# A cross-attention, linear-attention and mixture-of-experts layer on one core: half of each expert tile's down projection in split form, and slot-table writes in bursts

## The reference, cut to what matters

```python
x = x + xattn(layernorm(x), ctx, ctx, mask)       # 16 heads, 257 context rows
x = x + attn(layernorm(x))                        # causal linear attention
x = x + ffn(layernorm(x))
def ffn(x):                                       # 1024 tokens of 512
    shared = silu(x @ shared_wg.T) * (x @ shared_wu.T) @ shared_wd.T
    scores = sigmoid(x @ gate_w.T)
    topw, topi = top_k(scores, 8); topw = topw / topw.sum(-1)
    # 64 experts, I = 256; each token visits 8 of them
    g = silu(buf @ expert_wg); u = buf @ expert_wu
    out_buf = (g * u) @ expert_wd                 # the down projection
    return shared + sum over the 8 of topw * out_buf[expert, pos]
```

## Time and profile before

| | |
|---|---|
| median of 3 runs | 1292.07 us (1289.84 to 1292.19) |
| profiled execution, its own time | 1291.37 us |
| its span, first to last instruction | 1289.4 us |
| TensorE busy | 1225.0 us, 95% of the span |
| VectorE busy | 733.9 us, 57% |
| ScalarE busy | 594.8 us, 46% |
| GpSimd busy | 395.2 us, 31% |
| mean granted TensorE clock | 0.991 |

### The profile page before, as it was taken

How to read it: one execution, slowest core, us unless ns; L and a number is a source line. 1 busy time by engine, 2 the same in 40 slices (tenths; PEclk the granted TensorE clock), 3 DMA queues, 4 the chain that set the end, 5 groups by cost and what they waited for, 6 DMA issues and landing times. The chain is left out here.

```text
span 1289.4 us, 31822 instructions
## 1 busy us (share of the span) xinstructions
PE 1225.0 (95%) x9830; PEld 923.9 (72%) x9831; DVE 733.9 (57%) x1509; ACT 594.8 (46%) x1184; POOL 395.2 (31%) x312
## 2 busy tenths in 40 slices
PE   5999999999999999999999789999999999999993
PEld 4887788787887887877786347766777676667661
DVE  4445665756656657566557746556555556655550
ACT  2453433433434434333342165566655656656551
POOL 0002012021021120210202324566554656756442
PEclk9999999999999999999999999999999999999997
DMA  6732110210201102101012277999999999999886
GB/s 223 288 117 45 51 37 19 69 36 12 76 19 50 38 19 69 36 19 58 13 50 68 74 264 252 314 314 342 302 297 283 308 330 333 347 283 317 260 236 106
DMA packets 67370, 205.44 MB, mean 159 GB/s; under 512 B 16064, under 2 KB 18496, under 8 KB 56913
## 3 DMA queue, kind: packets, MB, share of 16 engines
q1 hardware_dynamic: 43392, 159.78, 34.3%
q0 software_dynamic: 23888, 44.40, 16.5%
HBM read 177.32 MB, written 37.03 MB: 166 GB/s over the span
## 5 line engine op out<-in xcount | busy, mean ns | idle before, releaser
L982 PE MATMUL bank<-ch,wkh 128*128 128x256 f32 x512 | 157.2, 307 | 11.9 <-DVE cl L660 8.4
L566 ACT ACTIVATE kt<-bank,colb 128x256 f32<-128x256 f32 x128 | 60.7, 474 | 225.7 <-PE bank L984 225.7
L459 POOL TENSOR_TENSOR rstd<-vep,half 128x1 f32<-128x1 f32 x32 | 20.7, 647 | 462.2 <-DVE vep L641 462.2
L1650 PE MATMUL ebank<-guh,xth 128*128 128x512 f32 x380 | 154.8, 407 | 1.5 <-DVE xtl L1548 0.8
L1543 DVE TENSOR_TENSOR gul<-wgu,guh 128x2048 fp32r<-128x2048 f32 x54 | 123.8, 2293 | 56.9 <-ACT guh L1459 56.8
L1387 POOL DMA_INDIRECT xg<-xn_rows,ig x95 | 123.4, 1299 | 89.8 <-issue 64.7
L1652 PE MATMUL ebank<-guh,xtl 128*128 128x512 f32 x380 | 149.0, 392 | 0.0
L1651 PE MATMUL ebank<-gul,xth 128*128 128x512 f32 x380 | 148.3, 390 | 0.0
L983 PE MATMUL bank<-cl,wkh 128*128 128x256 f32 x512 | 145.0, 283 | 0.0
L984 PE MATMUL bank<-ch,wkl 128*128 128x256 f32 x512 | 144.9, 283 | 0.0
L1680 PE MATMUL ebank<-wd,ht 128*128 128x512 f32 x292 | 134.3, 593 | 0.8 <-ACT ht L1444 0.8
(11 more groups left out here) (242 smaller groups left out, 2466.5 us busy)
## 6 DMA issues: line engine op xcount, KB each, us to landing
wgu<-in_egu SPq DMA_DIRECT2D x54, 1024.0 KB, 8.7
wd<-in_edn SPq DMA_DIRECT2D x54, 512.0 KB, 6.5
sgu<-in_egu SPq DMA_DIRECT2D x17, 1024.0 KB, 9.0
craw<-in_ctx SPq DMA_DIRECT2D x32, 514.0 KB, 3.3
sdn<-in_edn SPq DMA_DIRECT2D x17, 512.0 KB, 5.7
wqkv<-in_wqkv SPq DMA_DIRECT2D x1, 3072.0 KB, 18.1
second_sums<-x1b SPq DMA_DIRECT2D x9, 256.0 KB, 3.9
xa<-in_x SPq DMA_DIRECT2D x8, 256.0 KB, 3.0
```

The source lines that it names most:

```text
L982: mm(out, wkh[:, c, w], h[:, c, :], start=c == 0, stop=False)
L1650: mm(out, ah[:, c, :], bh[:, c, :], start=c == 0, stop=False)
```

## The change

In stage B the first of the two products of each tile's down projection (`DS = 1` of `IC = 2` chunks) is done as three rounded products of high and low parts; the second stays in full precision. For that

- ACT: `h_turned` copies the first chunk rounded (`hth`) and the second as it is (`ht`), two copies of 128 columns in place of one of 256; a new `high_d(k)` rounds the first chunk of the item's down weights (128x512), once an item, between `silu(k)` and `turned(k+2)`
- DVE: a new `low_h(k-1)` makes the low part of the turned hidden tile (128x128 from PSUM), for each tile, between `scatter_rows(k-1)` and `hidden(k)`; a new `low_d(k)` makes the low part of the down weights (128x512), once an item, behind `low_gu(k+2)`
- PE: `down` waits for `low_d` and `low_h` of its item (`d_low`, `hT_low`) in place of `hT_copied`, then does three rounded products and one in full precision
- the shared expert's turned hidden tiles go to two other buffers (`sht`), and ACT waits once for the last shared sum's store (`s_kept`) ahead of the item loop

In stage A the 8 table writes of a tile go out one behind the other at step 8, without the wait for `s_kv`, and those of the last tile but one all at its `pos`. ScalarE's tiles are all written out (`written_out = NT - 3`), and 20 semaphore increments (`FILL = 20`) stand at the end of ScalarE's stage A. The new `FILL` has the name of an older constant, which `masks` reads, so that a masked context position would now be capped at -20; the mask of these inputs is true everywhere.

```diff
-PACE = ("v", "A3", "DEN1", "NUM1")
-PACED = K - 1 - len(PACE)
+FILL = 20
...
                 if front and WRITE <= s < WRITE + K:
-                    wait(pool, s_kv, 6 * (BT * t + b) + k, tick)
                     write(s - WRITE)
...
                 if n == "outproj":
-                    if type(t) is int and t == NT - 1:
-                        px_wait(pool, n, t)
-                        write(K - 1)
...
-                    for j in range(EARLY if t == NT - 1 else PACED):
+                    for j in range(EARLY if t == NT - 1 else K):
                         write(j)
-                if n in PACE and type(t) is int and t == NT - 1:
-                    px_wait(pool, n, t)
-                    write(PACED + PACE.index(n))
...
-            passes(act, per_batch, on_post, on_pre, on_shared, written_out=3)
+            passes(act, per_batch, on_post, on_pre, on_shared, written_out=NT - 3)
+            for _ in range(FILL):
+                act.sem_inc(tick, 1)
...
+DS = 1
...
             def h_turned(item, tile):
                 done(act, tile, "hT", item)
-                nc.scalar.copy(tile.ht[:, :, :], ht_ps[tile.half][:, 0:IC * P].rearrange("p (c n) -> p c n", c=IC)).then_inc(tile.s["hT_copied"], 1)
+                nc.scalar.copy(tile.hth[:, 0, :], ht_ps[tile.half][:, 0:P])
+                nc.scalar.copy(tile.ht[:, 0, :], ht_ps[tile.half][:, P:2 * P]).then_inc(tile.s["hT_copied"], 1)
...
+            def high_d(item):
+
+                act.wait_ge(s_wd[item.w], (item.wturn + 1) * 16)
+                nc.scalar.copy(wdh[item.par][:, :, :], wd[item.w][:, 0:DS, :]).then_inc(s_w["d_high"], 1)
...
+            act.wait_ge(d.s_kept, 16 * (SHA - KEEP))
...
                     halves(act, its[k - 1], h_turned)
-                    halves(act, its[k], silu)
+                    with act.If(its[k].valid):
+                        silu(its[k], tiles[0])
+                        with act.If(its[k].two):
+                            silu(its[k], tiles[1])
+                        high_d(its[k])
                     halves(act, its[k + 2], turned)
...
+            def low_d(item):
+
+                w_done(dve, "d_high", item)
+                V.tensor_tensor(wdl[item.par][:, :, :], wd[item.w][:, 0:DS, :], wdh[item.par][:, :, :].bitcast(F32), ALU.subtract).then_inc(s_w["d_low"], 1)
+
+            def low_h(item, tile):
+
+                done(dve, tile, "hT_copied", item)
+                V.tensor_tensor(tile.htl[:, :, :], ht_ps[tile.half][:, 0:DS * P].rearrange("p (c n) -> p c n", c=DS),
+                                tile.hth[:, :, :].bitcast(F32), ALU.subtract).then_inc(tile.s["hT_low"], 1)
...
                         scatter_rows(its[k - 1])
+                    halves(dve, its[k - 1], low_h)
                     halves(dve, its[k], hidden)
                     halves(dve, its[k + 2], low_x)
                     with dve.If(its[k + 2].valid):
                         low_gu(its[k + 2].i, its[k + 2].w, its[k + 2].par)
+                    with dve.If(its[k].valid):
+                        low_d(its[k])
...
                 done(pe, tile, "y_ready", item, 1)
-                done(pe, tile, "hT_copied", item)
-                for c in range(IC):
-                    last = mm(y_ps[tile.half][:, :], tile.ht[:, c, :], wd[item.w][:, c, :], start=c == 0, stop=c == IC - 1)
+                w_done(pe, "d_low", item)
+                done(pe, tile, "hT_low", item)
+                for c in range(DS):
+                    last = split_mm(y_ps[tile.half][:, :], tile.hth, tile.htl, wdh[item.par], wdl[item.par], c, IC)
+                for c in range(DS, IC):
+                    last = mm(y_ps[tile.half][:, :], tile.ht[:, c - DS, :], wd[item.w][:, c, :], start=False, stop=c == IC - 1)
                 last.then_inc(tile.s["down"], 1)
```

More of the change, by code:

```diff
@@ L1199, in __init__ @@
         self.xtl = [sb(f"xtl{i}_", [P, DC, P], F32R) for i in range(2)]
-        self.ht = sb("ht_", [P, IC, P])
         self.sg, self.h = sb("sg_", [P, I]), sb("h_", [P, I])
         self.s_g = [sem(f"rows_in{i}_") for i in range(NX)]
-        names = ("xT", "xT_high", "xT_low", "gu", "silu", "h_ready", "hT", "hT_copied", "down", "y_ready")
+        names = ("xT", "xT_high", "xT_low", "gu", "silu", "h_ready", "hT", "hT_copied", "hT_low", "down", "y_ready")
         self.s = {n: sem(n + "_") for n in names}
@@ L1241, in stage_b @@
         etab = sb("etab", [1, P + 3], I32)
+        wdh, wdl = ([sb(f"wd{n}{i}_", [P, DS, D], F32R) for i in range(2)] for n in "hl")
+        for tile in tiles:
+            tile.hth, tile.htl = (sb(f"h{n}{tile.half}_", [P, DS, P], F32R) for n in "hl")
+            tile.ht = sb(f"ht{tile.half}_", [P, IC - DS, P])
+        sht = [tiles[1].ys[j][:, 0:I].rearrange("p (c n) -> p c n", c=IC) for j in range(2)]
         TAB2, TAB3 = 4 * (P + 1), 8 * (P + 1)
@@ L1252, in stage_b @@
         s_go, s_gone = sem("scatter_begun"), sem("gather_begun")
-        s_w = {n: sem(n) for n in ("gu_high", "gu_low")}
+        s_w = {n: sem(n) for n in ("gu_high", "gu_low", "d_high", "d_low")}
         tick = sem("tick_b")
@@ L1482, in shared_ht @@
                     act.wait_ge(s_sd, j - 1)
-                nc.scalar.copy(tiles[j % 2].ht[:, :, :], xt_ps[j % 2][:, 0:I].rearrange("p (c n) -> p c n", c=IC)).then_inc(s_shTc, 1)
+                nc.scalar.copy(sht[j % 2], xt_ps[j % 2][:, 0:I].rearrange("p (c n) -> p c n", c=IC)).then_inc(s_shTc, 1)
             def blank(xg):
@@ L1709, in shared_down @@
                 for c in range(IC):
-                    last = mm(sd_ps[j % 2][:, :], tiles[j % 2].ht[:, c, :], sdn[:, c, :], start=c == 0, stop=c == IC - 1)
+                    last = mm(sd_ps[j % 2][:, :], sht[j % 2][:, c, :], sdn[:, c, :], start=c == 0, stop=c == IC - 1)
                 last.then_inc(s_sd, 1)
```

## The result

The changed kernel takes 1331.5 us (median of 4 executions, 1325.1 to 1337.1) where the kernel before takes 1291.9: a ratio of 1.031, with a 95% interval from 1.027 to 1.035. The profiled execution is the fastest of the four, 1325.08 us with a span of 1323.2, 33.8 above the span before.

The account below looks back on a forecast made before the run. TensorE was taken to set the pace, with VectorE's chain to `down` nearly late. Waits 37.5 + loads 4.6 + end 0.4 - gaps 2 - saving 8.6 = 31.9 us on 1291.4, so 1324 as median; 8 in 10 from 1298 to 1345.

Parts of the forecast that it names:

- saving of the new products: Down projection: three rounded products replace one full-precision product, saving 0.09 us a tile, 8.6 for 95 tiles, 16 at most.
- waits for `low_h`: TensorE ahead of `down`: 28 waits, 37.5 us together, 8 of them behind a part's head.
- TensorE's own loads at heads: TensorE's item-number loads at a part's head, hidden before, show where `down` is released late: 4.6 us, 0 to 9.
- other gaps: TensorE's present gaps, 5.2 us in 780 to 1265, come from late weights; a slower pace removes 2.
- the end: The last item's `down` waits for `low_h` too: 0.4 us more.
- recurrence: For each of 71 items, wait(k) = R - P - wait(k-1) if positive, 0.5 more in R where item k+2 has two tiles.
- R: Time from the `turn_x` start behind `gate_up(k)` until `low_h(k)` releases `down(k)`: 6.9 us, 8.3 behind heads of parts.
- P: Time from the `turn_x` start behind `gate_up(k)` until TensorE reaches `down(k)`: 5.5 us with one-tile neighbours.
- the semaphore's 0.1: Term of R: about 0.1 us from the end of `low_h` to TensorE's start.
- So `low_d` costs nothing there: At a part's head VectorE's number loads run while `low_d` does, so its 0.61 us adds nothing.
- the rival that the transfers set the pace: Transfers limit the items, so a later `down` pushes the weights later still: 1330 to 1345 us; 8 in 100.
- clock rival: Each of the 28 TensorE waits lowers the granted clock, costing 34 us more: 1358 us; 7 in 100.

Follow-up runs that it names:

- after_again: The changed kernel itself run once more, on the same chip as the variants compared with it: 1.0319 of the kernel before.
- no_written_out: The changed kernel with its bursts of table writes, but ScalarE's last two stage A tiles back in the loop and no 20 increments: 1.0588 of the kernel before.
- stage_a_only: The kernel before with only the stage A edits (bursts, ScalarE's tiles written out, 20 increments), down projection in full precision: 0.9993 of the kernel before.

## Why the prediction was right

The sign, the mechanism and nearly the size held: 1324 forecast, 1331.5 measured, 1325.1 in the profiled execution. The terms were less right than their sum, and that the sum came so near is in part luck: an under-sized saving and under-sized loads cancel. The loop can be taken apart by its 70 periods from one `turn_h` to the next: each is compared with the shortest of its kind, and what it has above that goes to the gaps recorded in it. A period is sorted by the tiles of its item, of the next and of the one that `turn_x` turns.

| term | forecast | measured |
|---|---|---|
| saving of the new products | -8.6 | -15.2 |
| waits for `low_h` | +37.5 in 28 | +38.7 in 28 |
| TensorE's own loads at heads | +4.6 | +11.9 |
| other gaps: of before that go, new small ones | -2 | -6.9 and +8.4 |
| the granted clock | 0 | in the rows above, 1.7 of them |
| sum | +31.5 | +36.9, as by the two rows |
| stage A | 0 | -3.2 |
| the end | +0.4 | +0.2 |

- **The saving was under-sized by 6 to 7 us.** From one `turn_h` to the next, without a wait, an item with one tile on each side takes 5.12 before and 4.95 after, the shortest of 19 each; a two-tile item followed by one-tile ones 7.05 and 6.75, of 10. Such differences for all kinds, each by its count, add to 15.2 (for one kind, seen once and only with a wait, the difference of its neighbours was taken). Most of the missed part is the start: `down`'s first product now begins 0.35 behind `turn_x` (787.94 to 788.29) where it began 0.43 behind it, as it is of another kind. The forecast counted the change of kind only as a cost (0.08 a tile, and there it was right: `down` takes 1.64, forecast 1.63). The 16 that were its bound were near.
- **The waits were right, by a recurrence that is not the one written down.** A recorded idle time begins at the modelled end of a record, 0.25 later than the next start could be (0.60 less 0.35), so the 28 waits in the loop are 30.5 + 28 x 0.25 = 37.5, and 38.7 by the periods. R away from heads was right to 0.1. P was 5.30 and not 5.5 (0.35 + 1.64 + 0.14 + 2.82 + 0.35), so TensorE came earlier and waited more: the saving of a product goes back into the wait. But done as the prediction states it, the recurrence gives 50 us in 32 waits. Its 37.5 needs the transposes of second tiles in P as well, 0.43 each where item k+2 or k+3 has two and 0.15 where item k has: then it gives 38 in 29, and 30 and 46 with R less and more by 0.3. And the semaphore's 0.1 can't be read from the earlier trace rows; `low_h` and its semaphore take 0.43 together (833.34 to 833.77) for a forecast of 0.38.
- **"So `low_d` costs nothing there" held to 0.2 us; the heads are of two kinds.** The head of the earlier trace rows lies in the middle of a turn, the one shown above is that of a turn. The same head before:

```profile
827.03 2.29 DVE L1543 TENSOR_TENSOR gul<-wgu,guh 128x2048 fp32r<-128x2048 f32 x1 [1.00 <-ACT guh L1459]
831.08 0.17 DVE L1557 COPY ig<-src_rows 128x2 int32 x1 [1.76 <-issue]
831.47 0.17 DVE L1563 COPY ia<-dst_rows 128x2 int32 x1 [0.22 <-issue]
831.65 0.42 DVE L1538 TENSOR_TENSOR h<-ebank,sg 128x256 f32<-128x256 f32 x1
```

  From `low_gu` to where `low_h` will stand it is 4.62 us there, and 4.79 in the changed kernel (828.55 to 833.34). Of `low_d`'s 0.61, 0.17 shows, and so it is on the mean of the 16 such heads before and after. In the middle of a turn the 4.17 to 4.26 of before, all but one of them, are 4.34 to 4.54. With the other terms that makes an R of 8.2 in the middle of a turn, as forecast, and 8.65 at its head (9.1 where item k+2 has two tiles). The chain of work at the head shown has the loads (DVEq, L1282) on both sides of `low_d`:

```profile
829.47 1.85 DVEq L1282
831.32 0.10 DVE wdl_ L1558
831.42 0.03 issue
831.46 1.09 DVEq L1282
```

- **TensorE's own loads were mis-sized**, the largest error of the sum. I put them at the middle of 0 to 9 us, and they are above the 9. The 12 gaps have 11.2, and 13.1 with 0.16 each for the modelled tail (1.02 less 0.86), where there were 1.4 in 2 before; by the periods 13.9 and 2.0. The 3.2 us of the forecast also don't come out of its rows: from `weigh`'s end at 1094.84 to 1098.35 it is 3.5. What `down` waited for last there was the copy of `h_turned`, which ended at 1095.09. The profile shows the gaps as issue alone:

```profile
910.38 1.02 PE L1707 MATMUL ebank<-wd,ht_ 128*128 128x512 f32 x2
913.05 0.44 PE L1688 MATMUL ebank<-cn,h 128*128 128x128 f32 x2 [1.66 <-issue]
```

- **The gaps of before** (recorded as 1.8 and 0.8 us behind `hidden` and `low_x`) went; new ones ahead of the first rounded product, of 0.3 at most, are recorded as 3.1 for 0.5 and cost 7.4 by the periods, as the modelled end of a record hides the first part of each. ScalarE waits for late weights 1.1 us in place of 12.6, and they land in 8.1 us for 8.7, as the slower pace asks less of the transfers. This also speaks against the rival that the transfers set the pace.
- **The clock rival was not nil.** In the items of the profiled execution one window of ten us is below full clock, the one behind the gap above (its granted clock is the third number from the end, 0.83 for 10 us, 1.7 us lost):

```profile
910.00:920.00 10.00, 8.07 (x28) 5.69 (x27) 4.90 (x8) 3.04 (x5) 6.73 (x4) 0.83 1.03 341
```

  after_again has three windows of 0.83, and two of 0.95 and 0.88. The four executions of the changed kernel took 1325, 1327, 1337 and 1336 us at mean clocks of 0.990, 0.988, 0.984 and 0.981; 0.9% of 1325 is 12 us, their whole spread. So the clock explains why the median is above the profiled execution, but that is argued from these four pairs and not shown by a run of its own.
- **Stage A** was called nothing and gave 3.2 us. Five of its turns are 0.5 us shorter each (by the starts of one product, 243.77 to 329.10, where it was 244.79 to 330.61) and the last 0.3, 2.8 in all; the first, which has no table writes in it, is not shorter. The bursts do it, by no_written_out. Why the turn is shorter without the waits for `s_kv` was not looked into. On the chip of stage_a_only the gain was lost again ahead of stage B and did not show in the median (-0.9 of 1301, interval from -2.5 to +0.5).
- **What the forecast didn't see at all** is that ScalarE's code in stage A decides over its loop in stage B. I costed the writing-out by what ScalarE does at that place. Without it the change would have cost 1.06.

## What to carry to other kernels

An operation that is put between a late producer and its consumer costs by its place in the order, not by the engine's busy share: work out the chain from the last release to the wait, and put new work where the engine waits now; here that shortened a loop that had grown by 37 us to one grown by 7, with the same instructions. For a saving, take the shortest undisturbed period of an item before and after, start to start; a busy time or a median hides it under the waits. When a loop's time jumps by some per cent after an edit elsewhere, compare the packets of the instruction queues and look for idle time marked issue at the loop's head before you look for a reason in the work, and look behind the loop's last item as well. A number read at one head of a loop holds for the heads of its kind: compare the same place before and after.

## What the runs showed of the hardware

- The code of a loop can be fetched again in every turn, and code far ahead of the loop can decide whether it is: 68 packets of queue 14 for 7, with ScalarE at a standstill for 4.3 to 6.3 us at eight heads of turns, and 18 to 19 us more behind the last item, where ScalarE goes through turns without work. One more ScalarE and one more VectorE operation an item, with a wait between the two of VectorE (129 packets), brought it back, for both engines.
- VectorE's loads of item numbers run while its operation in flight does, and on: a further operation of 0.61 us ahead of the copies delays them by 0.17 us (mean of 16 heads).
- Behind the loads at the head of a part two small copies of VectorE start 0.38 us apart, elsewhere 0.07.
- A rounded product starts 0.35 us behind the start of four transposes, a full-precision one 0.43.
- Gaps of TensorE of 1 to 2.6 us lowered the granted clock in some executions and places and not in others; which of them do was not found.
